# Attention values from seven block products, a rebuilt slot order, and normalising on ScalarE

## The reference, cut to what matters

```python
q = einsum('bsd,de->bse', hidden_states, wq).reshape(B, S, H, DQ)      # H = 32 heads
kv = einsum('bsd,de->bse', hidden_states, wkv)
k = kv[..., :H * DN].reshape(B, S, H, DN)
v = kv[..., H * DN:H * (DN + DV)].reshape(B, S, H, DV)
scores = einsum('bqhd,bkhd->bhqk', q[..., :DN], k) * scale            # causal mask, then softmax
attn = einsum('bhqk,bkhd->bqhd', probs, v).reshape(B, S, H * DV)
return einsum('bse,ed->bsd', attn, wo)                                 # DN = DV = 128
```

## Time and profile before

| | |
|---|---|
| median of three runs | 1115.97 us (1115.33 to 1119.7) |
| profiled execution, own time | 1114.89 us |
| its span, first to last instruction | 1113.1 us |
| TensorE busy | 1103.9 us, 99% |
| VectorE busy | 636.7 us, 57% |
| ScalarE busy | 441.9 us, 40% |
| GpSimd busy | 736.4 us, 66% |
| granted TensorE clock | 1.0 |

### The profile page before, as it was taken

How to read it: one execution, slowest core, us unless ns; L and a number is a source line. 1 busy time by engine, 2 the same in 40 slices (tenths; PEclk the granted TensorE clock), 3 DMA queues, 4 the chain that set the end, 5 groups by cost and what they waited for, 6 DMA issues and landing times.

```text
span 1113.1 us, 19568 instructions
## 1 busy us (share of the span) xinstructions
PE 1103.9 (99%) x5826; PEld 948.1 (85%) x5826; DVE 636.7 (57%) x1638; ACT 441.9 (40%) x1288; POOL 736.4 (66%) x1109
## 2 busy tenths in 40 slices
...
DMA packets 24970, 59.14 MB, mean 53 GB/s; under 512 B 3552, under 2 KB 3872, under 8 KB 24800
## 3 DMA queue, kind: packets, MB, share of 16 engines
q1 hardware_dynamic: 24928, 58.61, 16.0%
...
...
## 4 chain that ended last, share of the span: by engine, by line
PE 95%; DVE 2%; POOL 1%; ACT 1%; issue 1%; DMA 0%; SPq 0%; POOLq 0%
PE banks L173 29%; PE banks L175 29%; PE banks L174 28%; PE banks L1515 4%; PE banks L1506 2%; PE banks L1531 2%; PE banks L864 0%; DMA acc<-in_x 0%; PE banks L991 0%; DVE kT_lo L1286 0%; ACT kT_hi L1281 0%; DVE banks L1303 0%; DVE work L541 0%; POOL wv_lo L1218 0%; DVE st L520 0%
## 5 line engine op out<-in xcount | busy, mean ns | idle before, releaser
L1237 POOL TENSOR_SCALAR prob<-prob,inv 128x128 f32<-128x128 f32 x128 | 47.6, 372 | 237.0 <-DVE inv L1447 237.0
L1212 POOL TENSOR_TENSOR form_lo<-wqk_stage,form_hi 128x256 fp32r<-128x256 f32 x192 | 141.3, 736 | 16.0
L1460 DVE TENSOR_TENSOR acc<-acc,banks 128x512 f32<-128x512 f32 x128 | 87.6, 685 | 81.4 <-PE banks L175 80.4
L1419 ACT ACTIVATE prob<-prob,top 128x128 f32<-128x128 f32 (+1 forms) x256 | 115.1, 453 | 32.6 <-DVE top L1441 32.6
L173 PE MATMUL banks<-tT_hi,form_hi 128*128 128x512 f32 x256 | 105.1, 411 | 0.0
L1441 DVE CUSTOM_DVE_ANT_0 prob<-banks,mask 128x128 f32<-128x128 f32 (+1 forms) x256 | 80.9, 353 | 36.5 <-PE banks L175 36.3
L175 PE MATMUL banks<-tT_hi,form_lo 128*128 128x512 f32 x256 | 100.2, 391 | 0.0
L173 PE MATMUL banks<-wv_hi,xT_hi 128*128 128x512 f32 x256 | 100.2, 391 | 0.0
L174 PE MATMUL banks<-tT_lo,form_hi 128*128 128x512 f32 x256 | 99.9, 390 | 0.0
L175 PE MATMUL banks<-wv_hi,xT_lo 128*128 128x512 f32 x256 | 99.8, 390 | 0.0
L174 PE MATMUL banks<-wv_lo,xT_hi 128*128 128x512 f32 x256 | 99.7, 390 | 0.0
...
## 6 DMA issues: line engine op xcount, KB each, us to landing
...
```

The lines of the kernel that those rows point to most:

```text
L1212: nc.gpsimd.tensor_tensor(form_lo[:, part], src[:, :], as_f32(form_hi[:, part]), ALU.subtract).then_inc(form_ready, 1)
L1237: nc.gpsimd.tensor_scalar(prob[:, i, 0:P], prob[:, i, 0:P], inv[:, i, 0:1], 1.0, ALU.mult, ALU.mult)
L1419: ins = nc.scalar.activation(pr, pr, ACT.Exp, bias=top[:, n % 2, r:r + 1], scale=-1.0, accum_out=total[:, n % 2, r:r + 1])
L1460: nc.vector.tensor_tensor(acc[:, t, :], acc[:, t, :], turn_bank(steps, step), ALU.add).then_inc(w_added, 1)
```

## The change

The V and Y steps of the loop are gone. Instead, each group computes the values of heads 2 and 3 of its own and heads 0 and 1 of the next group together, with the seven-product scheme: Q(j, i), j = 0 or 1, serves the values of batches j and j + 2 and is a product of 12 matmuls of 256 columns; the token block is now the stationary operand, xT or tT, and a mixed form of wv the moving one. ScalarE copies P1 to u3v; VectorE combines the others; P2, P4, P5 and P3 are evacuated by two ScalarE copies of 256 columns and the step M(j, i) of VectorE. P4, P5 and P3 of them take the long banks. The last group, which has no next one, needs only P1, P6, P2 and P3. The values of heads 0 and 1 of group 0 come from four steps of 24 matmuls of 256 columns, ahead of the loop.

GpSimd makes the mixed forms of wv (`prepare_values`: four sums and seven blocks split into hi and lo, for each of two halves c of the contraction) and puts the forms of P5 and P3 in a part of xT that is not needed any more. It no longer normalises: R(p) now has a ScalarE part, two Copy activations with a scale. SPLITS is one list without reference to the slots. Two W steps of each group move to the last slot of the list, and the slots are written anew. Some small tiles of layer 0 move in SBUF. The waits of S are as before; O waits for M's results.

```diff
-AHEAD_V = 1, 3, 5, 7
+AHEAD_V = range(BATCH)
...
+MIDDLE_SLOTS = [
+    [("L", 0, P5), ("P", 0, P3), ("W", 0, 2), ("L", 0, P3), ("P", 1, P1), ("W", 0, 3)],
+    [("P", 1, P6), ("P", 1, P2), ("W", 0, 4), ("L", 1, P2)],
+    [("P", 1, P7), ("W", 0, 5), ("P", 1, P4)],
+    [("L", 1, P4), ("P", 1, P5), ("W", 0, 6), ("L", 1, P5), ("W", 0, 7)],
+    [("P", 1, P3), ("Q", 0, P1), ("L", 1, P3), ("Q", 0, P6)],
+    [("Q", 0, P2), ("P", 2, P1), ("M", 0, P2), ("Q", 0, P7)]]
 FIRST_SLOTS = [
...
-MIDDLE_SLOTS = [
-    [("L", 0, P5), ("P", 0, P3), ("V", 4), ("L", 0, P3), ("Y", 4), ("P", 1, P1), ("W", 0, 0)],
-    [("P", 1, P6), ("V", 5), ("P", 1, P2), ("W", 0, 1), ("L", 1, P2)],
-    [("P", 1, P7), ("V", 6), ("W", 0, 2), ("Y", 6), ("W", 0, 3)],
-    [("P", 1, P4), ("V", 7), ("L", 1, P4), ("P", 1, P5)],
-    [("W", 0, 4), ("W", 0, 5), ("L", 1, P5), ("P", 1, P3), ("W", 0, 6), ("W", 0, 7)]]
...
+    [("L", 0, P5), ("P", 0, P3), ("P", 1, P1), ("L", 0, P3)],
+    [("P", 1, P6), ("P", 1, P2)],
+    [("L", 1, P2), ("P", 1, P7), ("Q", 0, P1), ("P", 1, P4)],
+    [("L", 1, P4), ("P", 1, P5), ("Q", 0, P6), ("L", 1, P5)],
+    [("P", 1, P3), ("Q", 0, P2), ("L", 1, P3)],
+    [("M", 0, P2), ("P", 2, P1), ("Q", 0, P7)]]
 OUTER_SLOTS = [
-    [("P", 2, P4), ("W", 1, 0), ("L", 2, P4), ("P", 2, P5), ("W", 1, 1)],
-    [("L", 2, P5), ("P", 2, P3), ("W", 1, 2), ("P", 3, P1), ("W", 1, 3)],
-    [("L", 2, P3), ("P", 3, P6), ("W", 1, 4), ("P", 3, P2)],
-    [("L", 3, P2), ("P", 3, P7), ("P", 3, P4), ("W", 1, 5)],
-    [("L", 3, P4), ("W", 1, 6), ("P", 3, P5)],
-    [("L", 3, P5), ("P", 3, P3), ("W", 1, 7)],
-    [("P", 4, P1), ("L", 3, P3), ("P", 4, P6)],
-    [("P", 4, P2), ("V", 8), ("L", 4, P2), ("P", 4, P7), ("Y", 8), ("V", 9)],
-    [("P", 4, P4), ("V", 10), ("L", 4, P4), ("P", 4, P5), ("Y", 10), ("V", 11)]]
-LAST_SLOTS = [
-    [("P", 2, P4), ("L", 2, P4), ("P", 2, P5)],
-    [("L", 2, P5), ("P", 2, P3), ("P", 3, P1)],
-    [("L", 2, P3), ("P", 3, P6), ("W", 1, 0), ("P", 3, P2)],
-    [("L", 3, P2), ("P", 3, P7), ("W", 1, 1)],
-    [("P", 3, P4), ("L", 3, P4), ("P", 3, P5)],
-    [("L", 3, P5), ("P", 3, P3), ("W", 1, 2)],
-    [("L", 3, P3), ("W", 1, 3), ("W", 1, 4)],
+    [("P", 2, P6), ("Q", 0, P4), ("P", 2, P2), ("M", 0, P4)],
+    [("L", 2, P2), ("P", 2, P7), ("P", 2, P4), ("W", 1, 0), ("L", 2, P4), ("Q", 0, P5)],
+    [("M", 0, P5), ("Q", 0, P3), ("P", 2, P5), ("M", 0, P3), ("W", 1, 1), ("L", 2, P5), ("Q", 1, P1)],
+    [("P", 2, P3), ("Q", 1, P6), ("W", 1, 2), ("L", 2, P3), ("Q", 1, P2), ("W", 1, 3)],
+    [("M", 1, P2), ("P", 3, P1), ("W", 1, 4), ("Q", 1, P7), ("P", 3, P6), ("Q", 1, P4)],
+    [("M", 1, P4), ("P", 3, P2), ("W", 1, 5), ("L", 3, P2), ("P", 3, P7), ("P", 3, P4), ("L", 3, P4)],
+    [("Q", 1, P5), ("W", 1, 6), ("M", 1, P5), ("Q", 1, P3), ("W", 1, 7), ("M", 1, P3), ("P", 3, P5)],
+    [("L", 3, P5), ("P", 3, P3), ("P", 4, P1), ("L", 3, P3), ("P", 4, P6)],
+    [("P", 4, P2), ("L", 4, P2), ("P", 4, P7)],
+    [("P", 4, P4), ("W", 2, 0), ("L", 4, P4), ("P", 4, P5), ("W", 2, 1)]]
+LAST_SLOTS = MIDDLE_SLOTS[0:5] + [
+    [("Q", 0, P2), ("P", 2, P1), ("M", 0, P2), ("Q", 0, P3)],
+    [("P", 2, P6), ("M", 0, P3), ("P", 2, P2), ("Q", 1, P1)],
+    [("L", 2, P2), ("P", 2, P7), ("P", 2, P4), ("Q", 1, P6), ("L", 2, P4)],
+    [("Q", 1, P2), ("P", 2, P5), ("M", 1, P2), ("Q", 1, P3), ("L", 2, P5)],
+    [("M", 1, P3), ("P", 2, P3), ("P", 3, P1), ("L", 2, P3), ("P", 3, P6)],
+    [("P", 3, P2), ("W", 1, 0), ("L", 3, P2), ("P", 3, P7)],
+    [("P", 3, P4), ("W", 1, 1), ("L", 3, P4)],
+    [("P", 3, P5), ("W", 1, 2), ("L", 3, P5), ("P", 3, P3)],
+    [("W", 1, 3), ("L", 3, P3), ("W", 1, 4)],
     [("W", 1, 5), ("W", 1, 6)],
     [("W", 2, 0), ("W", 2, 1)]]
-FIRST = with_pairs(FIRST_SLOTS + INNER_SLOTS + OUTER_SLOTS, True)
-MIDDLE = with_pairs(MIDDLE_SLOTS + INNER_SLOTS + OUTER_SLOTS)
-LAST = with_pairs(MIDDLE_SLOTS + INNER_SLOTS + LAST_SLOTS) + [
+FIRST = with_pairs(FIRST_SLOTS + OUTER_SLOTS, True)
+MIDDLE = with_pairs(MIDDLE_SLOTS + OUTER_SLOTS)
+LAST = with_pairs(LAST_SLOTS) + [
...
 def adds(steps):
 
-    return [s for s in steps if s[0] == "W"]
+    return ([] if steps is FIRST else [("W", 0, 0), ("W", 0, 1)]) + [s for s in steps if s[0] == "W"]
...
-    return step[0] == "P" and step[2] in EVACUATED
+    return step[0] == "P" and step[2] in EVACUATED or step[0] == "Q" and step[2] in (P4, P5, P3)
...
+    elif steps is FIRST:
+        before = [("V", b) for b in AHEAD_V] + [("P", 0, i) for i in (P1, P6, P7)]
     else:
-        before = [("V", n) for n in (1, 2, 3)]
-        if steps is FIRST:
-            before = [("V", n) for n in AHEAD_V] + [("P", 0, i) for i in (P1, P6, P7)]
-    return len(before), before + [s for s in steps if s[0] in "PVW" and is_long(s) == long]
+        before = [("P", 0, P7), ("W", 0, 0), ("W", 0, 1)]
+    return len(before), before + [s for s in steps if s[0] in "PQW" and is_long(s) == long]
...
+NEXT_HEADS = forms(4, "scale", "S1", P1, "S3", "S2", P6)
+SPLITS = (
+    value_forms(1, "V1", "V24") + forms(1, P4, P5) + value_forms(1, "VS1", "VS3", "VS2", "V67") + forms(1, P3)
+    + value_forms(1, "VS4", "V35") + forms(2, *HEAD_BEGIN) + forms(2, P2, "S4", P7, P4) + WO[0:2] + forms(2, P5, P3)
+    + forms(3, *HEAD_BEGIN) + forms(3, P2) + value_forms(0, "V1") + forms(3, "S4", P7, P4, P5, P3)
+    + value_forms(0, "V24", "VS1", "VS3", "VS2") + forms(4, *HEAD_BEGIN) + value_forms(0, "V67")
+    + forms(4, P2, "S4", P7, P4) + value_forms(0, "VS4", "V35") + forms(4, P5, P3) + WO[2:4]
+    + forms(5, *HEAD_BEGIN) + forms(5, P2, "S4", P7))
+LAST_SPLITS = [task for task in SPLITS if task[0] == "form" and task[1] < GH or task[0] == "wv" and task[1] == 1
+               or task[0] == "wo"]
+AHEAD_SPLITS = (
+    value_forms(0, "V1", "V24", "VS1", "VS3", "VS2") + [("v", 0, None), ("v", 1, None)] + forms(1, *HEAD_BEGIN)
+    + [("v", 2, None), ("v", 3, None)] + value_forms(0, "V67", "VS4", "V35") + forms(1, P2, "S4", P7))
+PIECES = [("wv", 1, 0), ("wv", 1, 1)] + WO[0:2] + [("wv", 0, 0), ("wv", 0, 1)] + WO[2:4]
+LAST_PIECES = PIECES[0:2] + WO
+AHEAD_PIECES = 4
+QK_LOADS = {1: (2, 3), 5: (4, 5)}
...
-    LONG, SHORT, S, O = (0, 1), (6, 2, 3), 4, 7
+    LONG, SHORT, S, O = (0, 1), (3, 6, 2), 4, 7
...
+    def prepare_values(pool, turn, c, part, loaded, released, used):
+        a11, a21 = wvo_stage[:, 0, 0:HALF_G], wvo_stage[:, 0, HALF_G:]
+        a12, a22 = wvo_stage[:, 1, 0:HALF_G], wvo_stage[:, 1, HALF_G:]
...
+        if part == "VS1":
+            pool.wait_ge(vform_ready, ready + 2)
+            pool.sem_inc(wait_passed, 1)
+            add(a22, a21, a22, ALU.add).then_inc(vprep_done, 1)
...
+            if part == "V1":
+                for i in range(RING):
+                    pool.wait_ge(vo_loaded[i], loaded)
+                src, at, last = a11, (vf_hi[:, 0, c], vf_lo[:, 0, c]), P1
+            elif part == "V24":
+                src, at, last = two(wvo_stage[:, 1]), (vf_hi[:, 3:5, c], vf_lo[:, 3:5, c]), P4
+            elif part == "V67":
+                after("VS2")
+                src, at, last = two(wvo_stage[:, 0]), (vf_hi[:, 1:3, c], vf_lo[:, 1:3, c]), P7
+            else:
+                pool.wait_ge(vo_ready, released)
+                cols = slice(HALF + c * HALF_G, HALF + (c + 1) * HALF_G)
+                src, at, last = two(wvo_stage[:, 1]), (xT_hi[:, 0:2, cols], xT_lo[:, 0:2, cols]), P3
...
+            pool.sem_inc(wait_passed, 1)
+            nc.gpsimd.tensor_scalar(at[0], src, 1.0, 1.0, ALU.mult, ALU.mult).then_inc(vprep_done, 1)
+            after(part)
+            add(at[1], src, as_f32(at[0]), ALU.subtract).then_inc(vform_ready, 1)
+            if part == "V35":
+                pool.wait_ge(vform_ready, ready + 4)
+                pool.sem_inc(vo_ready, 1)
...
+        elif older[0] == "Q" and older[2] == P1:
+            pe.wait_ge(vp1_copied, g * 2 + older[1] + 1)
+        elif older[0] == "Q":
+            freed = {P6: U2, P2: C11_LO, P7: U3, P4: C21_LO, P5: C22_LO, P3: C12_LO}[older[2]]
+            pe.wait_ge(vmix_done, value_mixes(g, steps, older[1], freed))
...
+    def first_values(pe, b):
+        step = ("V", b)
+        wait_turn(pe, 0, FIRST, step)
+        for r in range(2):
+            cols = slice((2 * b + r) * P, (2 * b + r + 1) * P)
+            for k in range(KD):
+                ins = matmul3(nc, two(turn_bank(FIRST, step))[:, r], xT_hi[:, k, cols], xT_lo[:, k, cols],
+                              first_wv[0][:, k], first_wv[1][:, k], k == 0, k == KD - 1)
+        ins.then_inc(v_done, 1)
...
+    def value_product(pe, g, steps, j, i):
+        step = ("Q", j, i)
+        left, k0, half = {P1: ((xT_hi, xT_lo), 0, 0), P6: ((tT_hi, tT_lo), FT, 0), P2: ((xT_hi, xT_lo), FT, 0),
+                          P7: ((tT_hi, tT_lo), 2 * FT, 0), P4: ((tT_hi, tT_lo), 0, 0),
+                          P5: ((tT_hi, tT_lo), 3 * FT, 0), P3: ((xT_hi, xT_lo), FT, 1)}[i]
+        right = value_form(i)
```

(38 more changed lines are left out.)

321 lines of the change are left out of this document (188 added, 133 removed).

## The result

The changed kernel takes 1140.73 us (median of 4 runs, 1138.36 to 1143.8) against 1115.65 us of the kernel before: a ratio of 1.0227, 95% interval 1.0208 to 1.0246. Its profiled execution took 1139.37 us, 24.5 more than the one of before; the prediction's sum was 23.0 more.

What follows compares the result with a forecast made beforehand. The prediction took the loop to be bound by the sum of TensorE's issue intervals. Its terms, -10.4 - 0.9 + 7 x 4.75 + 1.0 = +23.0 us, gave a forecast of 1138 us, range 1118 to 1152.

Steps and rivals of the forecast that it cites:

- The matmuls, -10.4 us: Value products on TensorE: 768 matmuls of 512 columns become 1368 of 256, 10.4 us less, 1.65 per full group.
- Normalising on ScalarE, -0.9: Moving normalising from GpSimd to ScalarE, 0.75 us a pair, is hidden and returns only TensorE's 0.9 us of waits.
- GpSimd, 0: GpSimd's new value forms: at most 84 us per group, less than a group's 105, so no cost.
- S(12), 2.1: Score step opening slot 12 waits for P(3, P4)'s low part: chain 2.59 us, cover 0.57; 2.1 in groups 0 to 6.
- S(14), 1.4: Score step opening slot 14 waits 1.4 us a group for L(3, P3) in slot 13; 0 if VectorE is on time.
- P(2, P5), 1.0: Product in slot 8 waits 1.0 us a group for Q(0, P5)'s long bank, free after M(0, P5).
- W(1, 4), 0.25: Output step in slot 10 waits 0.25 us a group for Q(1, P2)'s bank, free after M(1, P2).
- Last group, +1.0: In the last group S(8) and S(12) wait for P4's low part, 1.07 rather than 0.6 us each, about +1.0.
- rival D: Granted clock falls to 1.2 GHz for the slot behind S(12): +56 us, 1190 and more; chance 2 in 100.
- Rival A: Only the S(12) chain costs, VectorE and ScalarE being on time elsewhere: +3.8, 1119.8 us; chance 17 in 100.
- Rival B: The saving stays, waits costing under 0.67 us a group: under 1110.4 us, 1104 with no wait; chance 9 in 100.
- Rival C: Each delay feeds the next, about 6.5 us a group or an unseen place: 1151 to 1161; chance 12 in 100.

Runs made afterwards that it cites:

- all covered and more: The same run as experiment 11: experiment 10's lists with three further moves of steps, 1109.44 us, 0.994.
- experiment 7: The kernel before with ScalarE normalising and nothing else: 1114.07 us, 0.9991.
- experiment 8: The changed kernel with ScalarE's normalising moved behind the next evacuation of its queue: 1169.2 us, 1.047.
- experiment 3: The changed kernel with W(1, 6) and Q(1, P5) moved from slot 12 to the end of slot 11, behind L(3, P4): 1122.99 us, 1.0069.
- experiment 4: The changed kernel with W(1, 6) alone moved from slot 12 to the end of slot 11, behind L(3, P4): 1130.51 us, 1.0136.
- Experiment 1: The changed kernel with W(1, 5) moved behind P(3, P4) within slot 11: 1137.53 us, 1.0191.
- Experiment 5: The changed kernel with P(3, P5) and W(1, 7) exchanged in slot 12: 1141.08 us, 1.0226.
- experiment 10: The changed kernel with slots 8 and 11 to 15 reordered to cover all four waiting places, normalising left in place: 1112.54 us, 0.9966.
- experiment 6: The changed kernel with W(1, 1) moved ahead of P(2, P5) in slot 8: 1138.66 us, 1.0197.
- experiment 11: Experiment 10's kernel with M(1, P2) moved to the end of slot 9 and, in the last group, two L steps moved earlier: 1109.44 us, 0.994.

## Why the prediction was right, by its own steps

- **The matmuls, -10.4 us.** Right. The intervals in the block products are 0.119, as the earlier trace rows had it. No run shows the 10.4 alone, but in the loop it can be worked out: in "all covered and more" the period is 105.15 with 0.83 of excess left in the slots (0.48 in 15, 0.17 in 12, 0.18 in 7 to 10), so 104.32 without it; the kernel before has 105.92 without its waits for prob (experiment 7). That is 1.60, forecast 1.65. The estimated interval by the Trainium skill ("TensorE: Matmul & The Clock Gate", section "Wait — 56ns, not 53.3ns?"), 109.2 ns for 256 columns, is 10 ns under the measured one.
- **Normalising on ScalarE, -0.9.** Right within the measurement (experiment 7). Its price was put at 0.75 a pair; the pair takes 0.81, since the two operations of 451 ns overlap. That it isn't behind the waits for kT_lo and qT_lo is shown by experiment 8 for its place in the changed kernel. Experiment 8 also shows how thin the cover is: behind one more evacuation it costs 28 us. The prediction's "hidden behind a whole slot" holds where ScalarE comes to it in time; in group 0 of experiment 7 it cost 1 us by what stood behind it.
- **GpSimd, 0.** Right. It is busy 70.95 of 108 us in the window, against "84 at most", and waits 169.8 us for TensorE ahead of the value splits. No block product waited for GpSimd's forms. The one wait printed for a tile named vf_lo (0.6 us, at 1120.14) is a W step's in the last group: it waits for an O step's low part (L1652), kept in that tile, as the kernel before does under the name wv_lo (0.2 us).
- **S(12), 2.1.** Right: 2.10. Its chain took 570.35 - 567.68 = 2.67 us from the end of P(3, P4)'s issue, against the 2.59 of the earlier trace rows. Experiments 3 and 4 show it to be chain less cover where the cover comes from behind S(12): 1.36 us take 1.36 off the wait, and 2.8 us take all of it. Experiment 1 shows a second bound next to it, VectorE's own list, which the prediction had only as "some 0.1 late".
- **S(14), 1.4.** Right in kind, too dear by 0.3: 1.11 (1.24 with the 0.13 behind it). The queues ran as laid out: P(3, P3) was combined at 584.45 and the low part done at 585.60, 14.1 and 15.25 after the start of slot 12 (14.1 and 15.35 in the prediction); TensorE would have come at 14.2, not 14.0. Experiment 5 puts its origin at P(3, P5)'s place behind W(1, 7), and experiment 10 shows that it goes when P(4, P2) lies ahead of S(14).
- **P(2, P5), 1.0.** Right: 0.95 (experiment 6). **W(1, 4), 0.25.** 0.35 (experiment 11).
- **Last group, +1.0.** Too dear: S(8) and S(12) wait 0.80 and 0.81 there against 0.48 each before, +0.65.
- **The total.** +23.0 forecast, +24.5 in the profiled execution. The four places cost 4.87 a group with their neighbours, not 4.75 (+0.8), the last group 0.35 less, and 1.6 is in no term: rival D in small. Here the granted clock did fall behind S(12), in one group of seven. It had 2 chances in 100 as a fall for a whole slot and none in this size. These make 25.1; some 0.5 stays unassigned.
- **The signs.** The waits for kT_lo (1.84 to 1.93), the block product's intervals and TensorE's 97% came as named; those for qT_lo are 0.9, not over 1. Two signs came out otherwise: one wait for prob (0.3, in group 0), and a granted clock under 1 in the loop, which was named as a sign of being wrong and cost 1.6 us.
- **Rival A** (only S(12) costs, 1119.8) falls by experiments 5 and 6: the other places are real. With S(12) covered and they alone left, experiment 3 still takes 1123. **Rival B** (the saving stays) describes the last two experiments: the saving is there as soon as the steps stand in an order that covers the hand-overs. **Rival C** (delays feed on) fell: slot 12 ends only 0.1 late behind the 2.1 of slot 11.

So the change loses 25 us, as forecast, by four places in its slot lists, not by the algorithm: with the places covered the block products and the normalising on ScalarE together save about 0.6%. Against the kernel before with the normalising alone (1114.07, experiment 7) it is 4.6 us, 0.4%. The kernel before was not searched for a better order in the same way.
